# A decoder layer on one core: scores of the cross attention in two float32r parts, two heads in the two halves of TensorE's rows

## What is computed

```python
q = (x @ Wq).reshape(B, N, 16, 16).transpose(0, 2, 1, 3)
k = (context @ Wk).reshape(B, M, 16, 16).transpose(0, 2, 1, 3)
v = (context @ Wv).reshape(B, M, 16, 16).transpose(0, 2, 1, 3)
scores = jnp.einsum('bhid,bhjd->bhij', q, k) * 16 ** -0.5
scores = jnp.where(context_mask[:, None, None, :], scores, max_neg)
attn = jax.nn.softmax(scores, axis=-1)
out = jnp.einsum('bhij,bhjd->bhid', attn, v)
return out.transpose(0, 2, 1, 3).reshape(B, N, 256) @ Wo
```

## Time and profile before

| what | us |
| --- | --- |
| median of 3 runs | 1218.95 (1217.62 to 1220.98) |
| the profiled execution, its span | 1218.4 |
| PE busy | 1139.0 |
| DVE busy | 954.2 |
| ACT busy | 612.3 |
| POOL busy | 371.0 |
| cross attention, from its first to its last scores | 538 to 973 |

### The profile page before, as it was taken

One profiled execution on the slowest core, in us unless ns is written; L12 is line 12 of the kernel. 1 busy time (PEld: TensorE's weight loads), 2 busy tenths in 40 slices (PEclk: granted clock), 3 DMA queues, 4 the chain that ended last, 5 costly groups with the idle time before them and its releaser, 6 DMA issues. The chain is left out here.

```text
span 1218.4 us, 29643 instructions
## 1 busy us (share of the span) xinstructions
PE 1139.0 (93%) x11668; PEld 685.0 (56%) x11669; DVE 954.2 (78%) x1745; ACT 612.3 (50%) x1166; POOL 371.0 (30%) x351
## 2 busy tenths in 40 slices
PE   7899899999999999879999999999999847999996
PEld 6566666676677777643443344334434334676665
DVE  5989968987888688788778778877889466677757
ACT  4332333334333333227777767777788722344443
POOL 2422255222522222113200320221100424556651
PEclk9899999999999999999999999999999978999999
DMA  7100026000400000025720580075050152121125
GB/s 242 48 1 2 2 51 111 2 2 1 82 1 2 1 2 2 1 59 83 151 35 9 105 157 2 8 141 95 2 212 2 53 139 93 61 65 61 63 60 210
DMA packets 62200, 73.64 MB, mean 60 GB/s; under 512 B 14352, under 2 KB 53392, under 8 KB 61440
## 3 DMA queue, kind: packets, MB, share of 16 engines
q1 hardware_dynamic: 58288, 61.56, 21.3%
q0 software_dynamic: 3792, 10.36, 2.8%
HBM read 52.86 MB, written 18.78 MB: 59 GB/s over the span
## 5 line engine op out<-in xcount | busy, mean ns | idle before, releaser
L1737 DVE TENSOR_REDUCE neg_max<-pS 128x1 f32<-128x1024 f32 x238 | 285.0, 1220 | 50.9 <-PE pS L1520 50.8
L1652 ACT ACTIVATE pt<-pR 128x512 f32<-128x512 f32 x512 | 286.3, 600 | 73.4 <-PE pR L1543 68.5
L1543 PE MATMUL pR<-qs,ks 100*32 100x512 bf16 x2048 | 192.4, 381 | 1.9 <-ACT pt L1652 1.6
L1520 PE MATMUL pS<-ks,qs 100*32 100x512 bf16 x1904 | 146.4, 378 | 3.4 <-DVE neg_max L1737 1.8
L1557 PE MATMUL b_pO<-pt,b_v 128*32 128x512 f32 x1024 | 135.0, 598 | 3.0 <-ACT pt L1652 2.3
L411 PE MATMUL pP<-w_feat,a_xT 128*128 128x512 f32 x244 | 116.4, 600 | 0.7 <-ACT w_feat L689 0.7
L1543 PEld LDWEIGHTS pR<-qs,ks 100*32 100x32 bf16 x2048 | 57.2, 96 | 93.7 <-issue 23.8
L301 POOL TENSOR_TENSOR kf<-kf,fsum 128x2048 f32<-128x2048 f32 (+1 forms) x17 | 58.1, 3420 | 163.8 <-DVE fsum L883 163.8
L301 POOL TENSOR_TENSOR qs<-qs,fsum 128x2048 f32<-128x2048 f32 (+1 forms) x17 | 58.5, 3446 | 141.2 <-DVE fsum L883 141.2
L716 ACT COPY qfT<-pT 128x512 f32<-128x512 f32 x64 | 37.2, 582 | 126.3 <-PE pT L439 126.3
L1399 POOL COPY qs<-max_rows 3x512 bf16<-3x512 bf16 x60 | 36.7, 611 | 210.1 <-ACT max_rows L1645 207.1
(11 more groups left out here) (353 smaller groups left out, 2145.0 us busy)
## 6 DMA issues: line engine op xcount, KB each, us to landing
ks<-k_scr SPq DMA_DIRECT2D x8, 768.0 KB
qs<-q_scr SPq DMA_DIRECT2D x24, 256.0 KB
k_scr<-f SPq DMA_DIRECT2D x18, 256.0 KB, 2.7
ks<-k_scr SPq DMA_DIRECT2D x8, 512.0 KB
ks<-in_L_ffn_w_dram SPq DMA_DIRECT2D x2, 2048.0 KB, 10.5
ks<-in_L_ffn_w_dram SPq DMA_DIRECT2D x4, 1024.0 KB, 9.2
ks<-y_rows SPq DMA_DIRECT2D x16, 256.0 KB, 5.3
cx<-in_ctx_dram SPq DMA_DIRECT2D x3, 768.0 KB, 12.4
```

Of the source, the lines that this page charges most:

```text
L1520: ins = pe.matmul(pS1[q:q + XV, slot, 512 * half:512 * half + 512], qs[0:KR, bass.ds(par, 1), h, P * t + q:P * t + q + XV].rearrange("r a ...
L1543: ins = pe.matmul(ring[bank][q:q + XV, :], ks[0:KR, bass.ds(par, 1), h, P * j + q:P * j + q + XV].rearrange("r a n -> r (a n)"), qs[0:KR, ...
L1652: nc.scalar.activation(pt[:, j % 2, i, :], ring[bank], ACT.Exp).then_inc(exp_done, 1)
L1737: nc.vector.tensor_reduce(neg_max[:, hg % 2, u // G, u % G:u % G + 1], pS1[:, u % 2, :], AX_X, ALU.max, negate=True).then_inc(max_done, 1)
```

## The change

Queries and keys become two parts in the 4-byte type float32r (`head_parts`, `lo_parts`; in the cross attention `parts` with 2 instead of 3). The first part is ACT's copy (in the linear attention POOL's), the second is the block minus the first, written by DVE itself; POOL's `split` in the cross attention is gone, and in the linear attention it has two operations instead of four. A head has 2 x 16 rows (both key parts by the first query part), 4 rows for mask and maximum, and 16 rows (first key part by second query part): `KR` = 52. Even heads lie on partitions 0 to 51, odd heads on 64 to 115, as `ks_r` and `qs_r` over the same memory as `ks` and `qs`. A matmul of scores has 128 weight columns, and the pair of heads follows one another.

A unit of scores by token is now two heads, 128 tokens and half the keys (512); DVE's maximum gives two numbers a unit, `neg_max` holds both halves, and `split_max` begins with the smaller of the two negated maxima. In scores by context both heads of a pair stand together, with a semaphore each for even and odd heads, and the unit by token comes after them instead of between them. The normed x of the next batch lies in `v_new`, no longer in `f`, which the parts fill.

```diff
+K_ROWS = ((0, 0, 2), (AUG_END, 0, 1))
+Q_ROWS = ((0, 0), (XD, 0), (AUG_END, 1))
+def unit_of(u):
+
+    return u // 4, u % 4 // 2, u % 2
...
-                    for half in range(2):
-                        for q in range(0, P, XV):
-                            ins = pe.matmul(
-                                pS1[q:q + XV, slot, 512 * half:512 * half + 512],
-                                qs[0:KR, bass.ds(par, 1), h, P * t + q:P * t + q + XV].rearrange("r a n -> r (a n)"),
-                                ks[0:KR, bass.ds(par, 1), h, 512 * half:512 * half + 512
-                                   ].rearrange("r a n -> r (a n)"), start=True, stop=True)
+                    for e in range(2):
+                        at = HALF * e
+                        ins = pe.matmul(pS1[:, u % 2, 512 * e:512 * e + 512],
+                                        qs_r[at:at + KR, b % 2, 2 * hg + pair, P * t:P * t + P],
+                                        ks_r[at:at + KR, b % 2, 2 * hg + pair, 512 * half:512 * half + 512],
+                                        start=True, stop=True)
                     ins.then_inc(s1_done, 1)
...
+                def scores_by_context(b, start, hg, j, pair, banks, ahead_of):
+                    for i in (2 * pair, 2 * pair + 1):
+                        bank_is_read(b, start, ahead_of["score", hg, j, i])
+                        if j == 0:
+                            wait(pe, m_copied, G * (G * b + hg - 1) + i + 1)
+                        at = HALF * (i % 2)
+                        ins = pe.matmul(ring[banks["score", hg, j, i]],
+                                        ks_r[at:at + KR, b % 2, 2 * hg + pair, P * j:P * j + P],
+                                        qs_r[at:at + KR, b % 2, 2 * hg + pair, :], start=True, stop=True)
+                        ins.then_inc(s2_done[i % 2], 1)
...
-                            for i in range(2):
-                                bank_is_read(b, start, ahead_of["score", hg, j, i])
-                                scores_by_context(b, hg, j, i, banks["score", hg, j, i])
-                                if i == 0:
-                                    for ahead, g, u in units[:1]:
-                                        scores_by_token(b + ahead, g, u)
+                            scores_by_context(b, start, hg, j, 0, banks, ahead_of)
+                            for ahead, g, u in units[:1]:
+                                scores_by_token(b + ahead, g, u)
...
-                    nc.vector.tensor_reduce(neg_max[:, hg % 2, u // G, u % G:u % G + 1], pS1[:, u % 2, :],
+                    t, pair, half = unit_of(u)
+                    nc.vector.tensor_reduce(neg_max[:, hg % 2, half, t, 2 * pair:2 * pair + 2],
+                                            pS1[:, u % 2, :].rearrange("p (e n) -> p e n", e=2),
                                             AX_X, ALU.max, negate=True).then_inc(max_done, 1)
...
-                    nm = neg_max[:, hg % 2]
-                    own.did(nc.vector.tensor_copy(max_parts[:, :, :, 0], nm))
+                    own.did(nc.vector.tensor_tensor(max_now[:, :, :], neg_max[:, hg % 2, 0], neg_max[:, hg % 2, 1],
+                                                    ALU.min))
                     own.wait()
-                    own.did(nc.vector.tensor_tensor(max_rest[:, :, :], nm, max_parts[:, :, :, 0], ALU.subtract))
+                    own.did(nc.vector.tensor_copy(max_parts[:, :, :, 0], max_now[:, :, :]))
...
-                def load_k(b, half, heads, done):
+                def load_k(b, half):
                     now = slice(512 * half, 512 * half + 512)
-                    for at, n in K_RUNS:
-                        sp.dma_start(ks[XD * at:XD * (at + n), b % 2, heads, now],
-                                     k_scr[b, 0:n].rearrange("c (d h) n -> (c d) h n", d=XD)[:, heads, now]).then_inc(done, 16)
...
+                    for e in range(2):
+                        for at, c, n in K_ROWS:
+                            sp.dma_start(ks_r[HALF * e + at:HALF * e + at + XD * n, b % 2, :, now].bitcast(F32),
+                                         rows_by_parity(k_scr[b, c:c + n], e)[:, :, now]).then_inc(k_loaded, 16)
```

More of the change, by code:

```diff
@@ new lines, in load_k_aug, with load_q @@
+                def load_k_aug(b):
+                    for e in range(2):
+                        sp.dma_start(ks_r[HALF * e + AUG:HALF * e + AUG_END, b % 2].bitcast(F32),
+                                     aug_scr[b].unsqueeze(1).broadcast_to([4, XH // 2, M])).then_inc(k_loaded, 16)
+                def load_q(b):
+                    for e in range(2):
+                        for at, c in Q_ROWS:
+                            sp.dma_start(qs_r[HALF * e + at:HALF * e + at + XD, b % 2].bitcast(F32),
+                                         rows_by_parity(q_scr[b, c:c + 1], e)).then_inc(q_loaded, 16)
@@ L1306, in store_k, with load_q_aug @@
+                def load_q_aug(b):
+                    for e in range(2):
+                        sp.dma_start(qs_r[HALF * e + AUG:HALF * e + AUG_END, b % 2].bitcast(F32),
+                                     q_aug[AUG:AUG_END, :].unsqueeze(1).broadcast_to([4, XH // 2, L])
+                                     ).then_inc(q_loaded, 16)
                 def store_k(b, half):
                     n = entry(b, "k", 2 * half)
-                    wait(sp, split_done, 2 * (n + 1))
-                    for c in range(3):
+                    wait(sp, emptied, prepared(b, ("k", 2 * half + 1)))
+                    for c in range(2):
@@ L1318, in store_q @@
[L1318 removed]
+                    wait(sp, emptied, prepared(b, ("q", 1)))
+                    for c in range(2):
                         sp.dma_start(q_scr[b, c].rearrange("(m p) n -> p m n", p=P),
[L1320 to L1321 removed]
+                                     parts[:, n % 2, c].bitcast(F32)).then_inc(stored[2], 16)
+                    wait(sp, stored[2], 32 * b)
@@ L1382, in _ @@
                                           wk_raw[:, s, :].rearrange("p (h d) -> p d h", h=XH)).then_inc(wk_turned, 1)
-                def split(b, kind, i, n):
-                    s, m = slot(b, kind, i), i % 2
-                    part = [parts[:, s, c, m, :].rearrange("p a n -> p (a n)") for c in range(3)]
-                    wait(pool, emptied, n + 1)
-                    nc.gpsimd.tensor_tensor(part[1], rest[:, :], zero[:, :].broadcast_to([P, 512]), ALU.add
-                                            ).then_inc(rounded, 1)
-                    wait(pool, rounded, nth_of(b, kind, i) + 1)
-                    nc.gpsimd.tensor_tensor(part[2], rest[:, :], part[1], ALU.subtract).then_inc(split_done, 1)
-                    wait(pool, split_done, nth_of(b, kind, i) + 1)
                 def place_maxima(b, i, n):
@@ L1589, in batch @@
                                 n += 1
-                            for i in range(2, G):
-                                bank_is_read(b, start, ahead_of["score", hg, j, i])
-                                scores_by_context(b, hg, j, i, banks["score", hg, j, i])
-                                if i == 2:
-                                    for ahead, g, u in units[1:]:
-                                        scores_by_token(b + ahead, g, u)
+                            scores_by_context(b, start, hg, j, 1, banks, ahead_of)
+                            for ahead, g, u in units[1:]:
+                                scores_by_token(b + ahead, g, u)
                             for kind, i in steps[early(steps):]:
```

279 lines of the change are left out of this document (132 added, 147 removed).

## The result

The changed kernel takes 1229.62 us (median of four runs, 1226.65 to 1238.82), the kernel before beside it 1218.65: ratio 1.010, interval 1.006 to 1.014. The forecast was 1201, range 1166 to 1222: wrong sign, and outside the range. The execution that the profile shows took 1238.82 (span 1237.1), the longest of the four; since it alone was traced, its 9 us over the median can't be located. All medians here are of fast runs: one run each of `b_order` (1953.80) and of `a_warm` (1612.09, the one that was profiled), at granted clocks of 0.56 and 0.65, are left out.

What follows compares the result with a forecast made beforehand. TensorE was taken to bound the cross attention, with a 2.47 us exponential cycle just under. Step gains of 18.3 us: 1218.4 - 18.3 + 0.3 = 1200.4, plus 0.55 gives 1201.0; range 1166 to 1222.

Steps and rivals of the forecast that it cites:

- the cycle: Cross attention: last exponential frees weighted values and a bank, then second score pair, then two exponentials; 2.47 us a step.
- plain steps: Cross-attention steps without small extra work: 2.63 us before, 2.60 forecast; gain 0.03, times 39 is 1.2 us.
- A pair costs 0.21: Score matmuls: two heads in row halves side by side, one pass at bf16 rate; about 106 us less TensorE work.
- Rival C: float32r not at the bf16 rate, or row halves in turn: a pair costs 0.43, +34 us, 1253; chance 0.13.
- heavy step: Cross-attention step with a 1.72 us keys, values, queries or output product: 4.32 to 3.94; gain 0.38, times 36 is 13.7.
- s = 0.13 a change: TensorE's cost in us per switch between row halves and column strips; 280 more switches, 37 us.
- Order of C and T: Cross attention: context scores (C) of a pair now together, maxima unit (T, 0.43 us) behind, entering the cycle after a late S.
- late S: Small piece of work late in a cross-attention step; it moves the bank ring by one and makes four division changes.
- V: TensorE's weighted values of the step before, in cross attention; 0.86 us, in column strips.
- late transposes: Cross-attention steps with four late transposes: 3.30 us before, 3.16 forecast; gain 0.14, times 31 is 4.3 us.
- turned: Cross-attention steps with the early turning of the maxima: 3.07 us before, about 3.1 forecast, no gain.
- D: Rival: dear changes of the array's division, s over 0.21: 1222 to 1249 at 0.3; chance 0.05.

Runs made afterwards that it cites:

- b_order: Kernel before with only the changed order: both context-score matmuls of a pair together, then the unit by token; 1223.58 us, ratio 1.003.
- a_warm: Kernel after with the token-score units at the linear attention's end computed three times as TensorE ballast; 1230.95 us, ratio to before 1.010.
- c_serial: Kernel after with both heads of a pair taken from the lower half of TensorE's rows; 1295.18 us, ratio 1.062.
- b_full: Kernel before with each four-strip bf16 score group as one whole matmul of 128 columns, 100 rows; 1241.28 us, ratio 1.017.
- a_tfirst: Kernel after with the first unit by token of a step ahead of the first pair of context scores; 1220.11 us, ratio to before 1.000.
- d_vlast: Kernel after with the previous step's weighted values behind the second score pair and second token unit, then the small step; 1269.36 us, ratio 1.039.
- c_tfirst_keep: Kernel after, first token unit ahead of first score pair, linear attention's last token units computed three times, first group's 16 twice; 1221.22 us, ratio 1.001.

## Why the prediction was wrong

**What bounds the kernel; the cycle.** Right, and the most useful part: a second limit of 2.47 lay under plain steps of 2.63. That cycle, made longer, now holds them.

**A pair costs 0.21.** Right in kind: one pass, halves side by side (`c_serial`: 0.46 against 0.23). Rival C fell. The Trainium skill, "FP8 and Floating Point Precision", section "TensorE Precision Notes", says that true FP32 takes four passes; the trace adds that float32r takes the time of one, 0.23 us.

**But not behind a change or a wait.** There it costs 0.34. This term was left out; 0.12 more, and twice in a heavy step, it is the whole miss of 4.19 against 3.94: 36 x 0.25 = 9.0 us. The bf16 matmuls of 100 rows in `b_full` don't show it, float32r in one half does. A weight load of 128 float32r columns takes 185 ns; one of bf16 takes 97 ns (whole-matmul kernel). Behind a change the next pair's load starts 0.11 us after the first one's, and the first matmul's record is longer by that much (0.49 to 0.50 us for 0.39); in `b_full` the load follows after 0.015 us and the record is 0.01 longer (0.391 for 0.380). That the load stands open where it can't run ahead is the explanation that fits; no run changes the load alone, so it isn't shown. The Trainium skill, "TensorE: Matmul & The Clock Gate", section "Weight-path perf modes — Fast Weight Load (FWL) and DoubleRow", says that a faster weight load applies to 128 columns of a type other than FP32; 97 against 185 agrees, if float32r counts as FP32 there, which the page doesn't say.

**s = 0.13 a change.** Right: 0.10 into strips and 0.15 out, in bf16 and float32r alike. The whole-matmul kernel prices the changes, with the wider bf16 loads, at 21 us. The Trainium skill, "TensorEngine Tiling (Array Packing)", section "Key Properties", which says that a new mode drains the engine, agrees; it was the one rule that spoke against the change.

**Order of C and T.** The step that failed most. I let C1 and T1 enter the cycle only after a late S. In fact C1 waits for the third exponential in every plain step, and T1 and V queue behind it. Plain: forecast 2.60, measured 2.84 (39 x 0.24 = 9.4 us); late transposes 3.33 for 3.16 (5.3 us); turned 3.23 for 3.1 (2.0); the last steps 2.67 for 2.60 (0.5). Not all of this is the order: the last steps have no T and are 0.07 over as well. What the order costs is what `a_tfirst` gives back, 0.17 in a plain step (2.67) and 0.25 in a late one (3.08); between the first two and the last three steps of the stage it is 13 us. So this cause is shown. I had asked which bank C1 waits for with the times of the kernel before, where TensorE is always late and the exponential long done. When TensorE gets thinner its waits become real, and then it counts what stands behind each.

**The clock.** Put at zero, with "a clock below 1.00 in the stage" as a sign against me; it came. In the profiled execution the 122 steps between the ends miss the forecast by 23 us (4.3 more for 18.3 less); the ends of the stage and what lies outside it are the rest. At the exit ballast shows the cause: with more work on TensorE the clock stays up and the time falls. At the entry the fall costs 3.3 us in the last product of the linear attention. It isn't a fixed price of the change: of the nine float32r kernels without ballast in the linear attention five had it between 530 and 540 us and four had not; `d_vlast`, one of the four, begins its first scores at 536.5 us, before the kernel before (537.4; after 542.2). Nor is it float32r's alone: the whole-matmul kernel, whose linear attention is that of before, had 0.83 in 530 to 540 us and V at 547.2; with the other order it had 1.00 and 543.6. Why the clock falls there in one kernel and not in another stays open, and so does the other 1.4 us of the entry's delay.

**Maxima, GpSimd, DMA.** Right. The maxima take 1.22 still (287.1 us in all, 285.0 in the earlier trace rows), the 18.8 us of L1388 and the like of L1391 are gone from POOL (371.0 to 312.5) and nothing came of it; a copy of maxima takes 0.609 (I had said 0.65 to 0.9), and no load was waited for.

**TensorE's busy time.** Forecast 350 to 365 us in the stage; it is 427.6 in the 447 us from 542 to 989, as much as before. An instruction's time holds its latency, and that of the score matmuls fell less than their slots did (163.6 and 120.8 us in all, from 192.4 and 146.2); the busy share is no measure of the work taken off. The exponentials' waits, forecast to stay near 68, rose to 103.8.

**The rivals.** The time fell where D was, for another reason: s was as forecast, and what I hadn't priced (0.11 behind a change or a wait, T1 ahead of V, the clock) was added on top.

## What to carry to other kernels

When a change makes the bounding engine's work thinner, forecast each step again as a cycle through the next engine, with every wait of the in-order program and everything that is queued behind it: of the 69 us of work that the forecast took off TensorE nothing arrived, and moving one unit ahead of a waiting matmul was worth 9.5. A placement that looks wasteful (V or S between two waits) may be the cover of a wait; each time work was moved out of such a wait it cost 17 to 44 us, more than any saving that it was moved for. And where an engine with a granted clock is left with gaps, look at the clock too; filling the gaps paid at one of two places.

## What was not expected of the hardware

- float32r: one pass, 0.23 us for 52 rows by 512 columns, two row halves side by side, while a true fp32 product of 512 columns is two instructions of 0.43.
- The first float32r pair (52 rows) behind a change of division or a wait takes 0.11 us more than later ones; a bf16 matmul of 100 rows takes 0.01 more.
- Where the kernel after ran at the lower clock level (1.2 GHz) in its last steps, V to C2 is 1.87 us (980.69 to 982.56) where it was 1.00 (975.31 to 976.30). 20 ballast matmuls in ten steps keep 970 to 980 us at 1.00 instead of 0.66.
- 0.001 of mean granted clock went with 0.71 us of 1220 over 67 runs of one kernel. It doesn't carry over as a price: `c_tfirst_keep` had 0.006 more clock than `a_tfirst` (0.980, 0.974) and was no faster (1221.2, 1220.1).
